# Values projection moved behind the next tile's first heads, first groups in halves, weights requested in steps

## The reference, cut to what matters

```python
x = src                                   # (8, 2048, 1024) float32, one 2048 x 1024 slice per core
z = layernorm(x)
q, k, v = z @ Wq + bq, z @ Wk + bk, z @ Wv + bv      # 8 heads of 128
# attention inside blocks of 64 tokens, per head
probs = softmax(q @ k.T * 128 ** -0.5)
x = x + (probs @ v) @ Wo + bo
h = square(relu(layernorm(x) @ W_fc.T))              # 4096 wide
y = h @ W_proj.T
x = x + spike_count(y) / 5                # a step function of y with 5 levels
```

## Time and profile before

| | us |
|---|---|
| time, median of 3 runs | 735.78 (735.48 to 736.87) |
| the profiled execution, its own time | 736.52 |
| its span, slowest core (core 2) | 735.0 |
| spans of all eight cores | 730.5 to 735.0 |
| PE busy on core 2 | 702.7 (96%) |
| DVE / ACT / POOL busy on core 2 | 370.6 / 195.4 / 26.7 |
| mean granted TensorE clock | 0.996 to 0.999 |

### The profile page before, as it was taken

One profiled execution on the slowest core, in us unless ns is written; L12 is line 12 of the kernel. 1 busy time (PEld: TensorE's weight loads), 2 busy tenths in 40 slices (PEclk: granted clock), 3 DMA queues, 4 the chain that ended last, 5 costly groups with the idle time before them and its releaser, 6 DMA issues.

```text
span 735.0 us, 10914 instructions; the slowest of 8 cores (730.5 to 735.0 us)
## 1 busy us (share of the span) xinstructions
PE 702.7 (96%) x3861; PEld 333.6 (45%) x3936; DVE 370.6 (50%) x644; ACT 195.4 (27%) x353; POOL 26.7 (4%) x53
## 2 busy tenths in 40 slices
PE   1989999999999999999999999999999999999996
PEld 1434454444454444444444444444444444444444
DVE  4223766576576666534655224556224646321476
ACT  3350560362065035221201332111332110332000
POOL 5000000000001000000000000000000000000000
PEclk9999999999999999999999999999999999999999
DMA  7999144356219999488312101221101121100011
GB/s 165 198 198 203 44 118 109 115 122 195 115 57 238 159 214 230 117 222 200 114 60 80 35 0 59 88 84 58 57 1 47 47 81 57 58 0 1 29 44 43
DMA packets 19060, 74.64 MB, mean 102 GB/s; under 512 B 2240, under 2 KB 2496, under 8 KB 16576
## 3 DMA queue, kind: packets, MB, share of 16 engines
q0 software_dynamic: 6768, 31.46, 22.6%
q1 hardware_dynamic: 9792, 34.08, 14.6%
q10 hardware_dynamic: 2448, 8.40, 2.9%
HBM read 82.33 MB, written 16.78 MB: 135 GB/s over the span
## 4 chain that ended last, share of the span: by engine, by line
PE 89%; DMA 6%; DVE 2%; issue 1%; POOL 1%; ACT 0%; DVEq 0%; SPq 0%; ACTq 0%; POOLq 0%
PE ps_m L307 30%; PE ps_y L376 29%; PE ps_m L268 11%; PE ps_m L280 8%; PE ps_m L294 7%; DMA wv_sb<-Wv 5%; PE ps_t L250 2%; DMA xr<-x 1%; PE ps_y L329 1%; PE ps_y L357 1%; DVE acc_sb L600 1%; POOL wq_sb L685 1%; POOL wk_sb L685 1%; PE ps_t L341 0%; DVE acc_sb L597 0%
## 5 line engine op out<-in xcount | busy, mean ns | idle before, releaser
L307 PE MATMUL ps_m<-xn2t,w_sb 128*128 128x512 bf16 x1000 | 222.9, 379 | 1.5 <-issue 0.3
L376 PE MATMUL ps_y<-w_sb,h_sb 128*128 128x512 bf16 (+1 forms) x1003 | 218.8, 376 | 1.1
L307 PEld LDWEIGHTS ps_m<-xn2t,w_sb 128*128 128x128 bf16 x1024 | 98.9, 98 | 117.5
L376 PEld LDWEIGHTS ps_y<-w_sb,h_sb 128*128 128x128 bf16 x1024 | 99.7, 98 | 114.8
L452 ACT ACTIVATE h_sb<-ps_m 128x512 bf16<-128x512 f32 x128 | 76.4, 597 | 240.9 <-PE ps_m L307 240.9
L590 DVE TENSOR_TENSOR h_sb<-h_sb 128x512 bf16<-128x512 bf16 x128 | 53.5, 424 | 122.1 <-ACT h_sb L452 122.1
L600 DVE SCALAR_TENSOR_TENSOR acc_sb<-ps_y,acc_sb 128x1024 bf16<-128x1024 f32 (+2 forms) x72 | 78.6, 1092 | 7.5
L268 PE MATMUL ps_m<-xnt,wq_sb 128*128 128x512 bf16 x248 | 60.6, 386 | 2.4 <-ACT xnt L435 1.4
L280 PE MATMUL ps_m<-wv_sb,xnt 128*128 128x512 bf16 x251 | 58.1, 386 | 3.9 <-DMA wv_sb<-Wv 3.4
L268 PE MATMUL ps_m<-xnt,wk_sb 128*128 128x512 bf16 x246 | 59.1, 380 | 1.2 <-issue 1.0
L597 DVE TENSOR_SCALAR acc_sb<-ps_y 128x1024 bf16<-128x1024 f32 (+2 forms) x18 | 19.6, 1091 | 78.8 <-PE ps_y L376 78.7
(11 more groups left out here) (47 smaller groups left out, 353.4 us busy)
## 6 DMA issues: line engine op xcount, KB each, us to landing
xr<-x SPq DMA_DIRECT2D x32, 512.0 KB, 6.6
xl<-x SPq DMA_DIRECT2D x28, 512.0 KB, 4.8
w_sb<-Wfc POOLq DMA_DIRECT2D x8, 1024.0 KB, 12.6
x<-xr ACTq DMA_DIRECT2D x16, 512.0 KB, 3.2
w_sb<-Wpr POOLq DMA_DIRECT2D x8, 1024.0 KB, 30.1
out<-xr POOLq DMA_DIRECT2D x12, 512.0 KB, 2.9
wq_sb<-Wq POOLq DMA_DIRECT2D x8, 256.0 KB, 16.4
wk_sb<-Wk POOLq DMA_DIRECT2D x8, 256.0 KB, 17.2
```

Source lines behind the costliest of these rows:

```text
L307: m = E.matmul(bank(key)[:], w1_sb[fc // 4][:, k0:k0 + 128], xn2t[t % 2][:, c * 512:(c + 1) * 512], start=(c == 0), stop=(c == 7))
L376: return E.matmul(out, h_sb[fc][:, tt * 128:(tt + 1) * 128], w2_sb[fc // 4][:, k0:k0 + n], start=(fc == 0), stop=(fc == 31))
```

## The change

- Order: block -1 now holds the 16 groups q, k of tile 0 alone. Block 0 holds q, k of tile 1 for heads 0 to 3, the eight v of tile 0, q, k of heads 4 to 7, and the eight v of tile 1 (32 groups). In block 0 `turn_p` starts at s = 11 and `values` at s = 13.
- LayerNorm steps: in block -1 statistics, rstd, scale and transposes lie at s = 3, 4, 5 and 6 plus a multiple of 3 (the transposes at 6, 9, 12, 15). In block 0 they lie at 14, 15, 16 and 18 plus a multiple of 4.
- Front: row blocks 1 to 3 are transposed into banks of their own (`ps_x`). The first three groups are computed in halves of 256 tokens: three first halves, with `turn_x(2)` and `turn_x(3)` between them, and then three second halves. VectorE scales row blocks 0 and 1 ahead of the statistics of 2 and 3. ScalarE runs a Ln on a constant at its start.
- Transfers: GpSimd waits for `xr[0]` instead of `xr[1]`; each Wq and Wk of head h from 2 on is requested when that of head h - 2 has landed, and the halves of Wv when Wk of heads 6 and 7 have. Rows 4 to 7 have four buffers of their own (`xs`), requested as Wk of heads 0 to 3 land. bo and rows 8 and 9 are requested when all of Wv has landed.

```diff
@@ -50,12 +50,14 @@
-def qkv_keys(p):
-    keys = []
-    for h in range(8):
-        keys += [("q", p, h), ("k", p, h)]
-    return keys + [("v", p, tt, half) for half in range(2) for tt in range(4)]
+def qk_keys(p, heads=range(8)):
+    return [(kind, p, h) for h in heads for kind in "qk"]
+def v_keys(p):
+    return [("v", p, tt, half) for half in range(2) for tt in range(4)]
@@ -64,7 +66,29 @@
 def block_keys(b):
-    return qkv_keys(b + 1) if b < 3 else [("up", 0, fc) for fc in range(EARLY_UP)]
+    if b == -1:
+        return qk_keys(0)
+    if b == 0:
+        return qk_keys(1, range(4)) + v_keys(0) + qk_keys(1, range(4, 8)) + v_keys(1)
+    if b < 3:
+        return qk_keys(b + 1) + v_keys(b + 1)
+    return [("up", 0, fc) for fc in range(EARLY_UP)]
+def turn_p_head(b, s):
+    h = (s - (11 if b == 0 else 3)) // 2
+    return h if b >= 0 and s % 2 == 1 and 0 <= h < 8 else None
+def values_head(b, s):
+    return turn_p_head(b, s - 2)
+HALVED = 3
 def main_order():
@@ -79,30 +103,36 @@
     return {k: n for n, k in enumerate(keys)}
-def ln_unit(b, s, first):
-    if b <= 2 and s >= first and (s - first) % 4 == 0 and (s - first) // 4 < 4:
-        return 4 * (b + 2) + (s - first) // 4
-    return None
+LN_STATS, LN_RSTD, LN_SCALE = 0, 1, 2
+def ln_unit(b, s, step):
+    first, apart = {-1: (3, 3), 0: (14, 4)}.get(b, (2, 4))
+    n, rest = divmod(s - first - step, apart)
+    return 4 * (b + 2) + n if b <= 2 and rest == 0 and 0 <= n < 4 else None
+def ln_turn(b, s):
+    return ln_unit(b, s, 3 if b == -1 else 4)
 LAST = [(2, 0, 512), (2, 512, 512), (3, 0, 512), (3, 512, 256), (3, 768, 256)]
-LN_STATS, LN_RSTD, LN_SCALE, LN_TURN = 2, 3, 4, 6
 def turn_order():
-    keys = [("x", i) for i in range(4)]
+    keys = [("x", 0)]
     for b in range(-1, 4):
         for s in range(len(block_keys(b))):
-            if (i := ln_unit(b, s, LN_TURN)) is not None:
+            if (i := ln_turn(b, s)) is not None:
                 keys.append(("x", i))
-            if b >= 0 and s % 2 == 1 and 3 <= s <= 17:
-                keys.append(("pt", b, (s - 3) // 2))
+            if (h := turn_p_head(b, s)) is not None:
+                keys.append(("pt", b, h))
     keys += [("x", i) for i in range(20, 32)]
@@ -152,6 +182,8 @@
     w2_sb = [at(f"w2_sb_{i}", a, 4096, BF16) for i, a in enumerate(w2_at)]
+    xs = [at(f"xs_{i}", W1A + 32768 + 4096 * i, 1024, F32) for i in range(4)]
     xl = [at(f"xl_{i}", WORK + 65536 + 4096 * i, 1024, F32) for i in range(2)]
@@ -170,6 +202,7 @@
     rsum = at("rsum", SMALL + 800, 4, F32)
+    table_sb = at("table_sb", SMALL + 832, 1, F32)
     ps_m = [e(nc.psum_tensor(f"ps_m{i}", [128, 512], F32)) for i in range(3)]
@@ -177,12 +210,14 @@
     ps_v = ps_y[1]
+    ps_x = [None] + [y.bitcast(BF16) for y in (ps_y[0][:, 512:1024], ps_v[:, 0:512], ps_v[:, 512:1024])]
     def sem(name):
...
     ld_xr = [sem(f"ld_xr{i}") for i in range(4)]
+    ld_xs = [sem(f"ld_xs{i}") for i in range(4)]
     ld_xl = [sem(f"ld_xl{i}") for i in range(2)]
@@ -197,6 +232,7 @@
     full_t, free_t = sem("full_t"), sem("free_t")
+    full_x, free_x = sem("full_x"), sem("free_x")
     full_s, free_s = sem("full_s"), sem("free_s")
@@ -229,7 +265,19 @@
             return xr[i], (ld_xr[i], 16)
-        return xl[i % 2], (ld_xl[i % 2], 16 * ((i - 4) // 2 + 1))
+        if i < 8:
+            return xs[i - 4], (ld_xs[i - 4], 16)
+        return xl[i % 2], (ld_xl[i % 2], 16 * ((i - 8) // 2 + 1))
+    def turned(i):
+        return (full_x, i) if 1 <= i <= 3 else (full_t, turn_no[("x", i)] + 1)
+    def turned_copied(i):
+        return (free_x, i) if 1 <= i <= 3 else (free_t, turn_no[("x", i)] + 1)
+    def turn_bank(i):
+        return ps_x[i] if 1 <= i <= 3 else ps_t[:]
     def ln_target(i):
@@ -245,11 +293,12 @@
                 E.wait_ge(gp_id, 2)
-            turn_free(("x", i))
+            if i == 0 or i > 3:
+                turn_free(("x", i))
             for c in range(8):
-                m = E.transpose(ps_t[:, c * 128:(c + 1) * 128],
+                m = E.transpose(turn_bank(i)[:, c * 128:(c + 1) * 128],
                                 xn[i % 2][:, c * 128:(c + 1) * 128], ident[:])
-            m.then_inc(full_t, 1)
+            m.then_inc(turned(i)[0], 1)
         def main_free(key):
@@ -259,7 +308,7 @@
             if h == 0 and kind == "q":
-                E.wait_ge(free_t, turn_no[("x", 4 * p + 3)] + 1)
+                E.wait_ge(*turned_copied(4 * p + 3))
             if p == 0:
@@ -269,6 +318,22 @@
             m.then_inc(filled(key)[0], 1)
+        def q_or_k_half(key, half):
+            kind, _, h = key
+            w_sb, loaded = (wq_sb, ld_wq) if kind == "q" else (wk_sb, ld_wk)
+            if half == 0:
+                E.wait_ge(loaded[h], 16)
+            if key == ("q", 0, 0):
+                E.wait_ge(*turned_copied(2 * half))
+                E.wait_ge(*turned_copied(2 * half + 1))
+            for c in range(8):
+                k0 = h * 1024 + c * 128
+                t0 = c * 512 + half * 256
+                m = E.matmul(bank(key)[:, half * 256:(half + 1) * 256], w_sb[:, k0:k0 + 128],
+                             xnt[0][:, t0:t0 + 256], start=(c == 0), stop=(c == 7))
+            return m
         def v_group(key):
@@ -298,7 +363,7 @@
             if fc == 0:
-                E.wait_ge(free_t, turn_no[("x", 16 + 4 * t + 3)] + 1)
+                E.wait_ge(*turned_copied(16 + 4 * t + 3))
             if t == 0 and fc % 4 == 0:
@@ -377,19 +442,26 @@
                             w2_sb[fc // 4][:, k0:k0 + n], start=(fc == 0), stop=(fc == 31))
-        for i in range(4):
-            turn_x(i)
+        turn_x(0)
+        turn_x(1)
+        for s, key in enumerate(block_keys(-1)[:HALVED]):
+            q_or_k_half(key, 0)
+            if s < 2:
+                turn_x(2 + s)
         for b in range(-1, 4):
             for s, key in enumerate(block_keys(b)):
-                if (i := ln_unit(b, s, LN_TURN)) is not None:
+                if (i := ln_turn(b, s)) is not None:
                     turn_x(i)
...
                     scores(b, s // 2)
-                if b >= 0 and s % 2 == 1 and 3 <= s <= 17:
-                    turn_p(b, (s - 3) // 2)
-                if b >= 0 and s % 2 == 1 and 5 <= s <= 19:
-                    values(b, (s - 5) // 2)
-                main(key)
+                if (h := turn_p_head(b, s)) is not None:
+                    turn_p(b, h)
+                if (h := values_head(b, s)) is not None:
+                    values(b, h)
+                if b == -1 and s < HALVED:
+                    q_or_k_half(key, 1).then_inc(filled(key)[0], 1)
+                else:
+                    main(key)
             if b >= 0:
@@ -422,18 +494,16 @@
             E.wait_ge(ve_var, i + 1)
-            if i == 0:
-                E.wait_ge(ve_eps, 1)
             E.activation(lnv[i % 2][:], mv[i % 2][:, 1:2], ACT.Ln,
...
         def turn_copy(i):
-            E.wait_ge(full_t, turn_no[("x", i)] + 1)
+            E.wait_ge(*turned(i))
             dst = ln_target(i)[:].rearrange("p (c t) -> p c t", c=8)
             E.copy(dst[:, :, (i % 4) * 128:(i % 4 + 1) * 128],
-                   ps_t[:].rearrange("p (c t) -> p c t", c=8)).then_inc(free_t, 1)
+                   turn_bank(i).rearrange("p (c t) -> p c t", c=8)).then_inc(turned_copied(i)[0], 1)
         def main(key):
@@ -471,20 +541,23 @@
         E.dma_start(out=bias_sb[:], in_=bias_h).then_inc(ld_bias, 16)
+        E.wait_ge(ve_eps, 1)
+        E.activation(table_sb[:], eps_sb[:], ACT.Ln)
         ln_rstd(0)
...
         turn_copy(0)
+        turn_copy(1)
         ln_rstd(2)
-        turn_copy(1)
         ln_rstd(3)
...
             for s, key in enumerate(block_keys(b)):
-                if (i := ln_unit(b, s, LN_TURN)) is not None:
+                if (i := ln_turn(b, s)) is not None:
                     turn_copy(i)
-                if b >= 0 and s % 2 == 1 and 5 <= s <= 19:
-                    value_copy(b, (s - 5) // 2)
+                if (h := values_head(b, s)) is not None:
+                    value_copy(b, h)
                 if key[0] != "v":
@@ -534,7 +607,7 @@
             if i >= 2:
-                E.wait_ge(full_t, turn_no[("x", i - 2)] + 1)
+                E.wait_ge(*turned(i - 2))
             E.tensor_scalar(xn[i % 2][:], src[:], mv[i % 2][:, 0:1], rstd[i % 2][:, 0:1],
@@ -615,21 +688,21 @@
         ln_scale(0)
+        ln_scale(1)
         ln_stats(2)
-        ln_scale(1)
         ln_stats(3)
         ln_scale(2)
+        ln_scale(3)
         E.wait_ge(ld_bias, 16)
         E.tensor_single_scalar(bqs_sb[:], bias_sb[:, 0:8], DKS, ALU.mult).then_inc(ve_bqs, 1)
-        ln_scale(3)
         for b in range(-1, 4):
...
                     softmax_shift(b, s // 2)
-                if b >= 0 and s % 2 == 1 and 3 <= s <= 17:
-                    p_copy(b, (s - 3) // 2)
+                if (h := turn_p_head(b, s)) is not None:
+                    p_copy(b, h)
                 if b >= 0 and s % 2 == 1 and s < 16:
```

(16 more changed lines are left out.)

## The result

The median of the changed kernel is 731.9 us (731.77 to 732.71, 4 runs) against 736.3 (735.48 to 736.87) of the kernel before in the same runs: ratio 0.9944, with the interval 0.9926 to 0.9961. The forecast was 732.7 in a range from 730.0 to 735.0. The profiled execution took 731.83.

What follows compares the result with a forecast made beforehand. Bound by PE, 96% busy on the slowest core. Core 4's front to 24.05, 22.5 of groups, 5.5 of transposes, 13.8 of v groups, 0.2 and a 665.9 tail gave 731.9 span, 732.7 us reported; range 730.0 to 735.0.

Steps and rivals of the forecast that it cites:

- Step 1: Wv behind the first heads: its wait and the slow clock after it go, 4.8 us on core 2, 0.74 on core 4.
- Step 2: Front: halves hide the LayerNorm of units 2 and 3; gain 3.5 us on core 2, 4.6 on core 4.
- T + 12.1: Front: forecast start of k of head 1, 12.1 us after T, the first transpose; bounds T + 10.9 and T + 13.2.
- Step 3: Block -1, LayerNorm steps three groups apart: PE waits 0.93 us at each of four transposes, 3.7 us in all.
- Step 4: Weights requested in steps: charged 0; last Wk lands at 43, or 50 with row loads, needed at about 50.
- Step 5: From block 0's scores on: unchanged tail, 664.5 us on core 2, 665.9 on core 4, plus eight v groups, 13.8.
- the tail as a constant of each core: Block 0's first scores to the end: each core keeps its old time, 664.5 us on core 2, 665.9 on core 4.
- a second assumption: Reported time: the median lies 0.74 us below the profiled execution, as before, taking 733.4 to 732.7.
- the second (halves bring little): Front: slow clock lasts longer or copies come late, saving 2.5 instead of 4.6 us; 734.8, chance 0.14.
- the third (weights starve): Block -1, q and k of heads 4 to 7: TensorE waits for weights, 4 us at 2.8 per request, 736.7; chance 0.08.
- the fourth (VectorE late in block 0): Block 0: VectorE late, +1.5 us, 734.2; chance 0.06.
- the first: Block -1 transposes: they don't wait, rstd not being held by the emptying copy; 3.7 us stay, 729.0, chance 0.12.

Runs made afterwards that it cites:

- e2: The changed kernel without halves: four sets of transposes, then whole groups from the first on; 735.32 us, ratio 0.9957 to the kernel before.
- e1: The changed kernel with statistics, rstd and scale of block -1 one position earlier, transposes unmoved; 729.65 us, ratio 0.9882 to the kernel before.
- e9: The kernel of e3, but SyncE requests bo and rows 8 and 9 without waiting for Wv to land; 742.38 us, ratio 1.0084 to the kernel before.
- e3: The changed kernel with the group order undone (eight v of tile 0 back in block -1), all else as changed; 740.19 us, ratio 1.0025 to the kernel before.
- e4: The changed kernel with all weights requested at once, without the waits on earlier heads' landings; 732.11 us, ratio 0.9917 to the kernel before.
- e8: The kernel before with the new group order and the LayerNorm positions it needs, row blocks 4 to 7 still through two buffers; 740.51 us, ratio 1.0061.

## Why the prediction was right

**Step 1** held: no core waits for Wv. **Step 2** held in size: T + 12.1 was forecast, 11.3 to 12.5 measured, 12.3 on the slowest core; e2 without the halves has 14.4 to 15.5. **Step 3**, the new wait of 0.93 from start to start, is there four times on every core, as PE idles of 0.77; group 3 to block 0 is 28.06 us on core 3 against the forecast 22.5 + 5.5. e1 shows it by its cause: moving statistics, rstd and scale, and nothing else, takes the waits away. That it is rstd behind the emptying copy that holds them, and not late statistics, is seen in the timeline: VectorE has the statistics of unit 4 by 24.7 and then stands 4.22 us for rstd.

**Step 4** held in the sum: the last Wk at 44.2 (43 forecast), no wait. Two errors partly cancel in the 44.2: the first Wq landed at 14.0 on core 3, not 12.0 (6.6 us behind its request instead of 5.0), and the others came one per 2.01 us. A later profile of the changed kernel has one wait of 0.75 for a Wq, on its core 0. The Trainium skill, "DMA: Bandwidth & Descriptors", section "Queues, rings and completion order", has the queues take turns on each DMA engine, packet by packet; it doesn't say that the shares are equal, as the prediction has it. The runs fit that sharing without singling it out: rows requested by SyncE delay the weights by a few us (e9), and nothing starves in the changed order. What the prediction didn't see is how near it was: with the 3.7 us of step 3 gone, the weights are waited for. **Step 5**: the tail with its eight v groups is 678.3 to 678.4 us on every core, 664.5 without them.

The step that was off is **the tail as a constant of each core**. Core 4's was 665.9 before, 1.4 above core 2's, and the sum carried that over. Two lines of the kernel before, the first for core 0, the second for core 4, both for 240 to 250 us (columns: length of the stretch, then busy and count of PE, PEld, DVE, ACT and POOL, then granted clock, DMA share, GB/s):

```profile
240.00:250.00 10.00, 10.00 (x48) 4.53 (x47) 7.38 (x10) 0.00 (x0) 1.06 (x2) 1.00 1.02 155
```

```profile
240.00:250.00 10.00, 9.91 (x44) 4.34 (x44) 8.16 (x10) 0.00 (x0) 1.07 (x2) 0.92 1.00 161
```

Core 4 was granted 0.92 of the clock in the mean of that stretch, and its eight o groups of block 2 take 14.80 us there and 13.98 on core 0. That is 0.8 us; cores 5 to 7 have it too (0.91 to 0.92), cores 0 to 3 don't, and no core of the changed kernel's profile has a tail that would hold it. Another 0.5 stands in block 0 of core 4:

```profile
74.75 0.69 DVE L528 BATCH_NORM_STATS2 stat<-xl 128x6 f32<-128x512 f32 x1 [1.55 <-DMA xl<-x]
...
77.91 0.27 PE L341 MATMUL ps_t<-ident,p_sb 128*128 128x128 bf16 x2 [0.27 <-DVE p_sb L559]
```

Rows 8 were late even in the old order, VectorE waited 1.55 us and p was late on PE. The changed kernel doesn't have that: its rows 8 landed at 66.0 on core 3 and are first read at 80.79. The prediction put this gain at zero. With 664.5 and the first transpose of 11.52, its sum gives 730.1 for core 3, and 730.2 was measured. The reported time came within 0.8 us of the forecast because a second assumption went the other way: the 0.74 us between the profiled execution and the median of before weren't there again. That it cancels half of the first error is luck. Of the rivals, the second (halves bring little) fell with e2, the third (weights starve) and the fourth (VectorE late in block 0) by the waits of PE, and the first by the four waits themselves.

## What to carry to other kernels

When work is moved along an order written out by hand, count for every producer how many groups lie between the step that waits in another engine's queue (here rstd behind an emptying copy) and its consumer; one group too few cost 0.93 us a time here, and moving the producer up cost nothing. A reordering and the requests that feed it are one change: the order alone made this kernel 0.6% slower than before, where the whole change made it 0.5% faster on the same chip; and taking the order alone out of the changed kernel (e3 against e4) cost it 1.1%. A wait of TensorE can cost more than its length: behind a stop of 4.1 us the clock took another 2.7 (e9). Once one wait is taken out, look which transfer had its slack from it.

## What wasn't expected of the hardware

- The first statistics, which wait for the first 512 KB of rows, start between 4.61 us (core 3, e2) and 7.93 us (core 0, third profile of the changed kernel), early and late on other cores in each execution. In the versions whose waits are the same on all cores the slowest core is among the late ones, and 2 us of a core's span hang on it. Why it varies wasn't tried.
- The mean granted clock fell to 0.91 or 0.92 in one 10 us stretch, with PE busy throughout, on cores 4 to 7 of one execution of the kernel before, and cost 0.8 to 0.9 us. Nothing in the rows says why.
- A stop of 1.81 us on PE left the clock at its full level; stops of 3.38 and 4.78 (e8) didn't. In between it went both ways: behind 3.04 us (core 5, e3) the granted clock was 1.00, behind 2.10 (core 6, e3) it was 0.83 in the stretch from 50 to 60 us.
